# A two-block sandwich-norm FFN kernel: GpSimd multiplies both halves' h in the units of seven products, left operands are split at a unit's head, and a few early products and down tiles change places

## The reference

```python
def _L0_attn_ref(x, w_gate, w_up, w_down):
    s = jax.nn.silu(jnp.einsum('bsh,ih->bsi', x, w_gate))
    k = int(0.5 * I)                                  # I = 1376
    _, idx = jax.lax.top_k(-jnp.abs(s), k)            # per token: the 688 smallest |s| become 0
    s = s with zeros at idx
    s = s * jnp.einsum('bsh,ih->bsi', x, w_up)
    return jnp.einsum('bsi,hi->bsh', s, w_down)

def _L0_ffn_ref(x, W_gate, W_up, W_down):
    return (silu(x @ W_gate.T) * (x @ W_up.T)) @ W_down.T

x = x + _layernorm(_L0_attn_ref(_layernorm(x), L0_attn_w_gate, L0_attn_w_up, L0_attn_w_down))
x = x + _layernorm(_L0_ffn_ref(_layernorm(x), L0_ffn_W_gate, L0_ffn_W_up, L0_ffn_W_down))
```

## Time and profile before

| | before |
| --- | --- |
| time, median of 3 runs | 719.76 us (719.27 to 720.15) |
| profiled execution, its own time | 720.74 us |
| its span from first to last instruction | 718.9 us |
| PE busy | 706.9 us (98%) |
| DVE busy | 582.4 us (81%) |
| ACT busy | 383.1 us (53%) |
| POOL busy | 248.4 us (35%) |
| granted TensorE clock, mean | 0.999 |

### The profile page before, as it was taken

The page is one execution under the profiler, slowest core; times in us unless marked ns, Lnnn a source line. Parts: engine busy times, 40 slices in busy tenths (PEclk is TensorE's granted clock), DMA queues, the critical chain, the costliest instruction groups (busy, mean ns, idle before and its releaser), DMA issues.

```text
span 718.9 us, 9847 instructions
## 1 busy us (share of the span) xinstructions
PE 706.9 (98%) x3181; PEld 594.8 (83%) x3181; DVE 582.4 (81%) x1013; ACT 383.1 (53%) x610; POOL 248.4 (35%) x377
## 2 busy tenths in 40 slices
PE   8999999999999999999999999999999999999997
PEld 7888878888888888888888887877887888877885
DVE  6789778888898888987789889998688988877443
ACT  5896577677677566776654335433354333323230
POOL 1423123332323323233232666613315665621001
PEclk9999999999999999999999999999999999999999
DMA  8641424223554435544332677244953533334341
GB/s 276 200 110 63 100 70 98 56 78 87 124 130 83 100 86 116 128 84 111 102 107 72 174 232 217 87 156 115 247 143 111 161 119 111 93 111 147 137 142 44
DMA packets 126214, 88.56 MB, mean 123 GB/s; under 512 B 66416, under 2 KB 106608, under 8 KB 126160
## 3 DMA queue, kind: packets, MB, share of 16 engines
q1 hardware_dynamic: 126160, 87.91, 45.0%
HBM read 49.87 MB, written 18.87 MB: 96 GB/s over the span
## 4 chain that ended last, share of the span: by engine, by line
PE 68%; DVE 11%; issue 8%; ACT 5%; POOL 4%; DMA 3%; SPq 1%; DVEq 0%; ACTq 0%; POOLq 0%
PE gu_ps L813 14%; PE y_ps L754 13%; PE gu_ps L740 11%; PE tr_ps L813 10%; PE tr_ps L740 8%; PE gu_ps L835 4%; PE tr_ps L835 3%; ACT junk L937 3%; POOL move L1795 2%; PE gu_ps L788 2%; PE tr_ps L788 2%; PE y_ps L835 1%; DVE below L1376 1%; POOL thr L1798 1%; DVE xstat L1247 1%
## 5 line engine op out<-in xcount | busy, mean ns | idle before, releaser
L937 ACT ACTIVATE junk<-absv,thr 128x1383 bf16<-128x1383 f32 x96 | 139.1, 1449 | 43.4 <-POOL thr L1798 42.5
L754 PE MATMUL y_ps<-down_hi,hT 128*128 128x512 f32 x352 | 109.1, 391 | 0.0
L1795 POOL TENSOR_SCALAR move<-sgn 128x1 f32<-128x1 f32 x80 | 41.8, 522 | 108.0 <-ACT junk L937 108.0
L754 PEld LDWEIGHTS y_ps<-down_hi,hT 128*128 128x128 f32 x352 | 66.1, 188 | 14.4
L754 PE MATMUL y_ps<-down_lo,hT 128*128 128x512 f32 x176 | 69.5, 395 | 2.2 <-DVE hT L1279 2.2
L740 PE MATMUL gu_ps<-gate_hi,xT 128*128 128x460 f32 (+1 forms) x232 | 67.7, 373 | 0.0
L740 PE MATMUL gu_ps<-up_hi,xT 128*128 128x460 f32 (+1 forms) x232 | 67.2, 371 | 0.0
L1777 POOL TENSOR_TENSOR yrstd<-yvar,half 128x1 f32<-128x1 f32 x32 | 23.5, 736 | 85.3 <-DVE yvar L1288 85.3
L1770 POOL TENSOR_TENSOR xrstd<-xvar,half 128x1 f32<-128x1 f32 x32 | 21.9, 685 | 77.1 <-DVE xvar L1251 77.1
L1818 POOL TENSOR_TENSOR prod<-prod,gate_lo_raw 128x512 f32<-128x512 f32 (+1 forms) x20 | 26.1, 1305 | 64.3 <-DVE prod L1509 64.3
L740 PEld LDWEIGHTS gu_ps<-gate_hi,xT 128*128 128x128 f32 x232 | 44.1, 190 | 5.0
(11 more groups left out here) (306 smaller groups left out, 1923.2 us busy)
## 6 DMA issues: line engine op xcount, KB each, us to landing
absv<-prod SPq DMA_DIRECT2D x64, 176.0 KB, 3.4
h_scratch<-prod SPq DMA_DIRECT2D x38, 256.0 KB, 2.8
xin<-x_scratch SPq DMA_DIRECT2D x18, 256.0 KB, 2.7
xres<-in_L_attn_x SPq DMA_DIRECT2D x16, 256.0 KB, 3.4
x_scratch<-xres SPq DMA_DIRECT2D x16, 256.0 KB, 2.5
xg_even<-xin SPq DMA_DIRECT2D x64, 64.0 KB, 2.6
up_lo<-h_scratch SPq DMA_DIRECT2D x8, 512.0 KB, 3.8
up_hi<-h_scratch SPq DMA_DIRECT2D x8, 512.0 KB, 4.4
```

The source lines that it names most:

```text
L754: last = nc.tensor.matmul(y_ps[:, :], h, w[:, c, :], start=(c == 0 and i == 0), stop=(c == JC - 1 and i == 2))
L937: nc.scalar.activation(junk[:, 0:I + PAD], absv[:, q, A0 - PAD:A0 + I], ACT.Sign, bias=thr[:, q:q + 1], scale=-1.0, accum_out=sgn[:, q:q + ...
L1795: stepped(nc.gpsimd.tensor_scalar(move[:, :], sgn[:, q:q + 1], sgn[:, q:q + 1], float((WINDOW - 1) ** 2) + 0.5, ALU.mult, ALU.is_gt))
```

## The change

On **PE** the transposes at the start go from 15 and 10 to 19 and 9. `down(j-2)` stands behind up product max((9-j)//2, 0) of tile j instead of max(6-j, 0): behind product 2 in tile 4 as before, in tile 5 behind product 2 (was 1), in tile 6 behind 1 (was 0), in tile 7 behind 1 (was 0), and behind 0 from tile 8 on as before. In **part one**, for tile 2 alone (SOON), `split_h_hi(2)` moves on ACT from the head of round 4 to round 3, ahead of `count(3, 4)`, and `split_h_lo(2)` on DVE from behind `find_below(3)` to ahead of it. In the **units of seven products**, `h0` moves from DVE to POOL, behind `h1` of the same unit, except in the last unit of a pass (`last_h0`, on DVE). In the first pass `left_lo(u+1)` moves in units 4 to 9 from behind `sum_u2(u)` to the head of the unit, ahead of `gate0(u)`, and `x_stats` too in units 4 and 10; in unit 10 the splits `tile_lo(0, 0)` and `tile_lo(0, 1)` stand ahead of `x_normalise`. At the **down tiles**, the two halves of the last unit's h are split in the other order, and in the first pass `y_stats` of the last tile but none (tile 23) is made in round 6 instead of 7, and its `add_residual` ahead of the last `right_lo` instead of behind it.

```diff
@@ part 1, places @@
+    SOON = range(4, 5)
@@ TensorE: down_tile @@
-                pe.wait_ge(lasth_lo, 2 * g + half + 1)
+                pe.wait_ge(lasth_lo, 2 * g + 2 - half)
@@ TensorE: order @@
-            keep_busy(15)
+            keep_busy(19)
             transpose_x(0)
-            keep_busy(10)
+            keep_busy(9)
...
-                    if n == max(6 - j, 0) and j < TILES - 1:
+                    if n == max((9 - j) // 2, 0) and j < TILES - 1:
                         down(j - 2)
@@ ScalarE: order @@
             for j in range(3, TILES - 1):
-                if 3 < j < LATE:
+                if 3 < j < LATE and j not in SOON:
                     split_h_hi(j - 2)
                 count(j - 1, 5)
...
                 count(j, 3)
                 normalise_y(j - 2)
+                if j + 1 in SOON:
+                    split_h_hi(j - 1)
                 count(j, 4)
...
             tile_hi(0, 2)
+            last_h_hi(0, 1)
             last_h_hi(0, 0)
-            last_h_hi(0, 1)
@@ VectorE @@
-            def h0(u):
+            def last_h0(u):
...
             def last_h_lo(g, half):
-                dve.wait_ge(lasth_hi, 2 * g + half + 1)
+                dve.wait_ge(lasth_hi, 2 * g + 2 - half)
...
+                if j in SOON:
+                    split_h_lo(j - 2)
                 find_below(j - 1)
-                if 3 < j < LATE:
+                if 3 < j < LATE and j not in SOON:
                     split_h_lo(j - 2)
                 find_top(j - 1)
...
+                if u in XU:
+                    x_stats(XU[u])
+                if D15 < u < JC - 1:
+                    left_lo(u + 1)
                 gate0(u)
                 if u == D15:
                     add_residual(last)
                 sum_u2(u)
-                if u in XU:
-                    x_stats(XU[u])
-                if u < JC - 1 and u != D15:
+                if u < D15:
                     left_lo(u + 1)
                 sum_u4(u)
-                if u in XU:
-                    x_normalise(XU[u])
                 if u == JC - 1:
                     tile_lo(0, 0)
                     tile_lo(0, 1)
+                if u in XU:
+                    x_normalise(XU[u])
                 gate1(u)
...
                 up0(u)
-                h0(u)
+                if u == JC - 1:
+                    last_h0(u)
+            last_h_lo(0, 1)
             last_h_lo(0, 0)
-            last_h_lo(0, 1)
...
-                y_stats(TILES + r)
+                if r < S_TILES - 1:
+                    y_stats(TILES + r)
...
                 for i in SUM_AT.get(r, ()):
                     right_sum(1, i)
+                if r == S_TILES - 2:
+                    y_stats(TILES + r + 1)
                 for i in R_AT.get(r, ()):
+                    if i == TSEQ[-1]:
+                        add_residual(TILES + r)
                     right_lo(1, i)
-                add_residual(TILES + r)
+                if r < S_TILES - 1:
+                    add_residual(TILES + r)
@@ GpSimd @@
+            def h0(u):
+                pool.wait_ge(silu0_done, u + 1)
+                pool.wait_ge(up0_done, u - PLAIN + 1)
+                at = s_part("sum0", u)[0:width(u), :]
+                nc.gpsimd.tensor_tensor(at, at, s_part("gate0", u)[0:width(u), :], ALU.mult).then_inc(h0_done, 1)
...
                 h1(u)
+                if u % JC < JC - 1:
+                    h0(u)
```

More of the change, by code:

```diff
@@ L1202, in _ @@
             tile_hi(S_TILES, 2)
+            last_h_hi(1, 1)
             last_h_hi(1, 0)
-            last_h_hi(1, 1)
             tile_hi(S_TILES + 1, 0)
@@ L1733, in _ @@
                 up0(u)
-                h0(u)
+                if u == UNITS - 1:
+                    last_h0(u)
+            last_h_lo(1, 1)
             last_h_lo(1, 0)
-            last_h_lo(1, 1)
             tile_lo(S_TILES + 1, 0)
```

## The result

| | before | changed |
| --- | --- | --- |
| median | 719.79 us (4 runs, 719.27 to 720.15) | 724.33 us (4 runs, 722.94 to 725.70) |
| ratio to before | | 1.0061 (95%: 1.0049 to 1.0073) |
| profiled execution, span | 720.74, 718.9 | 722.94, 721.1 |

The change makes the kernel slower by 0.6%, 4.5 us. 720.2 was predicted and 722.0 was the end of the range; "slower" had 0.21. The profiled executions differ by only 2.2: that of before lies 1.0 above its median, that of the changed kernel is the fastest of its four. The loss lies ahead of down tile 1: from that tile's start to the end of the span it is 224.9 and 224.2 us in the two profiles of before, and 224.2, 224.3 and 224.9 in the three of the changed kernel.

The account below looks back on a forecast made before the run. PE, busy 706.9 of 718.9 us, was taken as the bound, DVE as setting the first pass's pace. 0 + 1.3 - 0.8 + 0 = +0.5 on the median 719.76 gave 720.2 us, range 716.4 to 722.0.

Parts of the forecast that it names:

- +1.3: Units of seven products, first pass: longer DVE cycles and the pass's end together start down tile 1 1.3 us later.
- -0.8: Tile 23, unit 11: y_stats a tile earlier removes PE's wait for the residual, 0.8 us gained, at worst 0.3.
- the 0 of part one: Tile 2's early split and later down products: lead of 0.5 left, taken as 0 since DVE sets the first pass's pace.
- The price of T to gate0: First-pass units: from up0's end (T) to the next gate0, h1's rest, left split and h0 in a row, 3.86 us.
- Two of 10.0 and two of about 9.7: DVE's four cycles from T(5) to T(9), 39.4 us against 37.8 before, so T(9) comes 2.4 later.
- the term of x_stats, -1.05: End of first pass, unit 10: x_stats with its small instructions runs under the wait for gate0, saving 1.05 us.
- Unit 5: ACT's copy of M1 waits for a store; gate0(5) stands behind the late split, 3.5 later, T(5) 0.9 later at 442.0.
- The tightest is tile 10: Part one, low splits from tile 6 on: tile 10 has slack 2.0, asked for 1.5 + 1.0, so 0.5 is lost.
- The distance of 0.98 from the median: Kernel before: its profiled execution stands 0.98 us above the median; subtracted to turn the profiled forecast into a median.
- Rival 1: First-pass units: h0 hidden on POOL, overlapping the left split, cycle under 9.53; gains 3.0 to 4.2 us; chance 0.31, faster.
- Rival 2: First-pass units: POOL's late sums delay left_hi and left_lo, cycle 10.4, time 721.8 to 722.3; chance 0.21, slower.
- Start, second pass and tail: 0: Transposes at the start, the second pass's units and the tail behind the last matmul: each answered with nothing, 0.

Follow-up runs that it names:

- left_one: Changed kernel with the low parts of units 7 to 10, first pass, made by a one-input scaled copy, subtraction left out: 721.29 us, ratio 1.0014.
- store_first: Changed kernel with the stores of unit 3's h issued ahead of the six down-weight loads instead of behind them: 722.17 us, ratio 1.0030.
- u_soon: Changed kernel with tile 2's early split alone taken back, the later down products kept: 722.89 us, ratio 1.0043.
- u_part1: Changed kernel with tile 2's early split and the later down products both taken back: 722.94 us, ratio 1.0041.
- best_a: Kernel before with only the transposes at the start, the swapped halves of the last h and tile 23's earlier norm: 720.30 us, ratio 1.0003.
- u_left: Changed kernel with the left split, x_stats and x_normalise taken back to their old places, h0 still on POOL: 725.41 us, ratio 1.0065.

## Why the prediction was wrong

**The sign.** A loss of 0.5 was forecast as the sum of +1.3, -0.8 and several zeros. The mechanism behind the +1.3 was right; its size was not (2.9 in the first pair of profiles). Of the others the -0.8 was a chance of the profile, and the 0 of part one did not hold.

**The price of T to gate0 was right.** 3.86 forecast, 3.70 measured, in units 6 to 8 of all three profiles; T(5), forecast at 442.0, was 441.96. The waits of 0.2 to 0.6 before product 3 of units 7 to 9 came as well (0.23, 0.63, 0.26).

**The cycle was mis-sized.** "Two of 10.0 and two of about 9.7", 39.4 from T(5) to T(9): measured 40.4 in all three profiles (10.1, 10.5, 10.1, 9.7). Three things are in it. The rest of the cycle, gate0 to T, was taken as what remains when the split is subtracted, 6.16; it is 6.43. The split's 2.34 had overlapped its neighbours: from sum_u2 to sum_u4 it was 2.87 with the split between them (443.20 to 446.07) and is 0.78 without, so it had taken 2.09. Unit 7 took 0.4 more: sum_u2 starts 1.17 after gate0 there and 0.80 in the others. Why stays open. The product that it reads, M6, was done at 451.8, five us before, so it was not PE; and the same 1.17 stands at the same instruction in all eight profiles of kernels with the changed order of DVE in units 6 to 10, left_one among them, where PE waited before no product 3. And of the two cycles of "about 9.7, where POOL has fewer sums" the first was 10.14: POOL's sums met no split any more, since they now run behind h0, so there was nothing to save. The second came out at 9.67 for another reason: unit 10 has 96 rows, its split 1344 numbers instead of 1792, and T to gate0 is 3.24. T(9) came 3.5 late in the first profile and 3.8 in the third, instead of 2.4 (6.5 in the second, which had the low clock and the longest unit 5).

**The end of the pass was mis-sized by 0.5.** From T(9) to tile 1 the sum had -1.05; it was -0.5. Gate0(10) cost +0.7 (0.6 forecast) and the swapped halves gave 0.5 (0.6 forecast). What failed is the term of x_stats, -1.05: with it gone from the read-out of unit 10, gate0 to the start of up0 fell from 8.39 to 7.67, by 0.7. In before, sum_u4 had started 1.65 after sum_u2 with x_stats between them, and it starts 0.78 after it without: 0.9, not 1.05; the two splits of down tile 0, now ahead of x_normalise, take 0.2 back.

**Unit 5 was right in the forecast and worse in another execution.** The copy's wait for the store decides it; T(4) to T(5) was 12.5, 13.3 and 12.4. store_first shows the loads ahead of the stores as its cause: 10.2 with the stores first.

**Part one: a zero that did not hold.** The steps up to down(4) came about as written: search 1.5 later, waits of 0.7 and 0.2 where 1.0 and 0.5 were forecast. The step that failed is "The tightest is tile 10". Only low splits of h were compared. The low split of x for tile 8 hangs on the same search, through `select` and the transposition before it on DVE, and was ready in the kernel before at 178.75 for a PE that came at 179.62: 0.9 to spare against 2.0. The changed kernel waits 1.5 to 1.8 us there. And "in the first pass DVE sets the pace, and I take 0" failed too, in part: u_soon's profile keeps its 1.3 to 1.9 from tile 8 until tile 1, while u_part1's loses a lead of 0.7 in unit 5. The early split alone loses more than a lead: T(2), the first of the units of seven, is 407.3 to 408.2 in the five profiles of kernels with the new start and without the early split, and 408.8 to 411.1 in the nine with it. By the medians it costs 1.4 to 2.2 in the changed kernel. That PE's clock can be lower behind such a wait, 1.5 more, stood in no step.

**Tile 23: -0.8 from one profile.** Against that profile it came (no wait, 0.7 gained). The second profile of before hasn't the wait, and best_a got nothing at the median.

**The distance of 0.98 from the median was taken as a constant.** It was one execution's: 0.2 in the second profile of before, -1.4, +1.6 and -1.1 in those of the changed kernel.

**The rivals.** Rival 1 (h0 hidden) is refuted by the 3.07 us of h0, which are 1.29 in u_left, where the split stands elsewhere. Rival 2 had the right sign, but its mechanism didn't happen: left_hi was done before the split in every unit from 6 on, and the sums ran undisturbed.

**Start, second pass and tail: 0 held.** The first product begins 1.0 earlier (7.95 against 8.96), and the next is stopped for the low part of the weights (0.4), as written. In the second pass h0 takes 3.08 in units 12 to 18 too, but in the three profiles PE waits at most 0.2 us in them, and the time from tile 1 to the end is the same as before.

What stays open is why single executions of the changed kernel range from 722.9 to 726.2 us. One of three profiles had the low clock (1.5), and cycle 5 differs by 0.9; these give about 2.4 of the 3.2, but they were seen in profiles and not in the other runs. Open too is the 0.4 of unit 7, and how far the costs of the two places depend on one another.

## What to carry to other kernels

Moving a multiply from DVE to POOL saves DVE nothing if the next DVE instruction has both operands in SBUF and the one after that needs the product: count the three in a row, and take what surrounds them from start to start, since durations overlap. When a search or another serial chain is delayed, list everything that hangs on it and take the least slack among all of them, not among the operands the edit is about. A wait that is worth 0.8 us in one profile should be seen in a second one before it is entered as a gain.

## What was not expected of the hardware

- A wait of PE of 1.8 us was followed by 3 us at the lower granted clock (0.50) in one profile, and eight other profiles with waits of 1.5 to 2.0 at the same place had none; a wait of 3.2 us was followed by 3.3 us at 0.51, in a kernel whose six runs all lie within 0.35 us.
- A `tensor_scalar` of DVE with a single SBUF input, at twice the split's speed, stopped POOL's multiply as the two-input split did (2.15 us, of which 1.16 lie behind the copy's end, against 1.29 undisturbed).
- Two stores issued behind six weight loads landed 8.4 us after their issue, where the same stores of other units took 2.3 to 5.0; issued ahead of them the copy that waits for them began 2 us earlier.
